# Two dense graph products: byte counts moving past a stationary float32r table, in place of bf16 counts stationary and a bf16 table moving

## What is computed

```python
# layer A: Gaussian mixture convolution over edges, then SiLU, residual and layer norm
gauss  = exp(sum_a(-0.5 * (attr - mu)**2 / (EPS + sigma**2)))         # edges x 3
msg    = einsum('eko,ek->eo', (x[src] @ g).reshape(E, 3, 64), gauss)
aggr   = segment_sum(msg, dst) / max(cnt, 1)
x      = layernorm(x + silu(aggr + x @ root_w + bias + x))
# layer B: two SAGE convolutions over the same edges
def sage(h, W_self, W_neigh, b):
    mean = segment_sum(h[src], dst) / max(deg, 1)
    return h @ W_self + mean @ W_neigh + b
h      = relu(sage(x, W_self1, W_neigh1, b1))
x      = layernorm(x + sage(h, W_self2, W_neigh2, b2))
```

## Time and profile before

| | us |
|---|---|
| median of 3 runs (8571.0 to 8632.7) | 8616.2 |
| span of the profiled execution, first to last instruction | 7138.9 |
| of it up to the end of the count stage | about 5273 |
| fix-up, layer A's end, table | about 194 |
| dense product n = 0 | 827 |
| dense product n = 1 with the end | 845 |

### The profile page before, as it was taken

One profiled execution on the slowest core, in us unless ns is written; L12 is line 12 of the kernel. 1 busy time (PEld: TensorE's weight loads), 2 busy tenths in 40 slices (PEclk: granted clock), 3 DMA queues, 4 the chain that ended last, 5 costly groups with the idle time before them and its releaser, 6 DMA issues.

```text
span 7138.9 us, 141917 instructions
## 1 busy us (share of the span) xinstructions
PE 4916.9 (69%) x35195; PEld 3933.0 (55%) x35196; DVE 4364.6 (61%) x15089; ACT 2701.0 (38%) x8318; POOL 3409.5 (48%) x3146
## 2 busy tenths in 40 slices
PE   1466666666666655566666665565647999999999
PEld 1123444444444433444444444444437999999999
DVE  5667787777777776777777766666645222222222
ACT  3112554554555543455554455555532000000000
POOL 5013776677766665677777777777720000000000
PEclk5556888888888887788888878888867999999999
DMA  3001222222222222222222222222234999999998
GB/s 77 30 25 48 92 83 92 82 97 97 78 95 78 96 78 72 94 96 96 95 77 96 95 97 87 91 94 97 96 92 157 382 380 383 380 368 385 384 385 341
DMA packets 258332, 1082.60 MB, mean 152 GB/s; under 512 B 140102, under 2 KB 144230, under 8 KB 194406
## 3 DMA queue, kind: packets, MB, share of 16 engines
q1 hardware_dynamic: 139588, 965.46, 34.6%
q0 software_dynamic: 100352, 102.96, 6.4%
q10 hardware_dynamic: 18120, 11.31, 0.7%
HBM read 751.67 MB, written 327.81 MB: 151 GB/s over the span
## 4 chain that ended last, share of the span: by engine, by line
PE 39%; DVE 19%; issue 14%; POOL 11%; DVEq 10%; ACT 4%; DMA 2%; ACTq 0%; SPq 0%; POOLq 0%
PE pw L983 22%; POOL rE L498 11%; PE pw L809 9%; DVE rE L1283 5%; PE pw L834 3%; DVEq L1316 3%; DVEq L1492 2%; DVE rE L1343 2%; PE pw L781 2%; DVE rE L1281 2%; ACT rE L545 2%; DVE rE L1411 1%; ACT rB L584 1%; DMA rE<-in_x,idx 1%; DVEq L1268 1%
## 5 line engine op out<-in xcount | busy, mean ns | idle before, releaser
L498 POOL DMA_INDIRECT rE<-in_x,idx x3136 | 3407.4, 1087 | 1828.5 <-issue 1745.6
L809 PE MATMUL pw<-rE 128*128 128x193 f32 x7824 | 1688.3, 377 | 863.1 <-DVE rE L1343 810.2
L584 ACT CAST rB<-pw 128x792 bf16<-128x792 f32 x1568 | 1257.2, 813 | 2509.8 <-PE pw L834 1151.1
L809 PEld LDWEIGHTS pw<-rE 128*128 128x128 f32 x7824 | 1539.5, 222 | 1064.5 <-DVE rE L1343 985.5
L545 ACT ACTIVATE rE<-rE,cols 128x64 f32<-128x64 f32 x4704 | 1255.4, 345 | 8.1 <-DMA tab<-tab_d 8.1
L834 PE MATMUL pw<-rE 128*128 128x396 f16 x3840 | 809.8, 358 | 487.1 <-DVE rE L1283 440.6
L1283 DVE TENSOR_SCALAR rE<-iperm,gr 128x392 f16<-128x392 f16 x3840 | 1051.3, 313 | 0.1
L834 PEld LDWEIGHTS pw<-rE 128*128 128x128 f16 x3840 | 370.1, 103 | 865.9 <-DVE rE L1283 532.0
L983 PE MATMUL pw<-rB,rA 128*128 128x192 bf16 x9604 | 810.7, 246 | 0.1
L983 PE MATMUL pw<-rE,rA 128*128 128x192 bf16 x9604 | 810.5, 246 | 0.1
L983 PEld LDWEIGHTS pw<-rB,rA 128*128 128x128 bf16 x9604 | 790.7, 98 | 1.6
(11 more groups left out here) (258 smaller groups left out, 2550.8 us busy)
## 6 DMA issues: line engine op xcount, KB each, us to landing
rA<-count SPq DMA_DIRECT2D x392, 1568.0 KB, 8.4
count<-rB SPq DMA_DIRECT2D x98, 3136.0 KB
rE<-in_x,idx POOLq DMA_INDIRECT x3136
cols<-cols_d SPq DMA_DIRECT2D x98, 64.0 KB
cols_d<-rA SPq DMA_DIRECT2D x3, 1568.0 KB, 5.2
rA<-in_edge_attr ACTq DMA_DIRECT2D x1, 4608.0 KB
out<-gcol ACTq DMA_DIRECT2D x97, 32.0 KB, 5.7
count<-rB SPq DMA_DIRECT2D x8, 224.0 KB, 2.0
```

Source lines behind the costliest of these rows:

```text
L498: pool.indirect_dma_start(out=gath[:, s, u * CB + b, :], out_offset=None, in_=x, in_offset=bass.IndirectOffsetOnAxis(ap=idx[:, s, u * CB + ...
L584: act.copy(stage[:, s, :, j * 2 * W:(j + 1) * 2 * W].rearrange("p h (w n) -> p w h n", w=2), pu[j % 3][:, :, 0:CW].rearrange("p w (h n) -> ...
L809: ins = pe.matmul(sums[side][:, 0:AW], onehot[:, side, bb, :], wgath[:, side, bb, :], start=(bb == 0), stop=(bb == CB - 1))
```

## The change

Counts become bytes. `stage` is uint8 with four slots, and ScalarE's cast of L584 writes bytes. The bound columns of `comp` hold 1/16 and 1/2048 instead of 1, so that their sums fit a byte, and the limit becomes 240. `count` is laid out by chunks of TC = 4 destination tiles: [4 planes, chunk, 128, ROWB], in which a partition's row is sixteen blocks (`SPANS`: fourteen of 6 groups of src, two of 7), each block holding 4 tiles x 6 (or 7) groups x 128 counts. A tile is stored with two DMAs of runs of 768 and 896 bytes. The fix-up makes three digits by shifts of an int32, and stores each with two DMAs; GpSimd clears a slot of `stage` beforehand.

The table has two pieces instead of three, in float32r: the value with its low 12 bits cleared, and the rest, so `TW` is 128. Now the table is the stationary operand, [128 src, 2 x 64], and the counts of 4 tiles move, 512 columns; the sum is [2 x 64, 512 dst], transposed. [...]

The epilogue runs on a chunk of four tiles: `summed` adds the own rows' pieces, `turn` transposes two tiles at once, ScalarE copies the 512 columns of sums and 256 of own rows (`copied_out`), and `apply` makes eight f32 products of 64 columns. The stacked neighbour weights add the two pieces. 1 / degree is applied behind it, as is the bias, on 256 elements. Output DMAs are issued by GpSimd, one for four tiles. The first block groups of n = 1 are widened while the last two chunks of n = 0 are finished.

```diff
-TW = 3 * D
+TC = 4
+NC = (NT + TC - 1) // TC
+TW = 2 * D
-PARTS = ((0, 26), (26, 24), (50, 24), (74, 24))
+PARTS = ((0, 24), (24, 24), (48, 24), (72, 26))
+SPANS = [(6 * b, 6) for b in range(14)] + [(84, 7), (91, 7)]
+GROUPS = 4
+SHARE = ([3 if b in (3, 7, 11, 13) else 4 for b in range(16)],
+         [3 if b in (2, 3, 6, 7, 10, 11, 13) else 4 for b in range(16)])
...
-                sp.dma_start(tile_of(count[part][0], ORDER[q] - PARTS[part][0]), stage[:, q % 2, None, 0:NT, :]).then_inc(a_st[q % 2], 16)
+                c, t = divmod(ORDER[q] - PARTS[part][0], TC)
+                sp.dma_start(sixes(part)[:, 0, c, t], stage[:, q % 2, 0:84, :].rearrange("p (b h) n -> p b (h n)", h=6)).then_inc(a_st[q % 2], 16)
+                sp.dma_start(sevens(part)[:, 0, c, t], stage[:, q % 2, 84:NT, :].rearrange("p (b h) n -> p b (h n)", h=7)).then_inc(a_st[q % 2], 16)
...
+            def load_counts(part, c, n):                       # SyncE
+                for g in range(GROUPS):
+                    with sp.Fori(0, planes, 1) as pl:
...
+                        for b in range(4 * g, 4 * g + 4):
...
+                            sp.wait_ge(d_conv, free)
+                            sp.wait_ge(a_conv, free)
+                            sp.dma_start(cring[:, b % 4, None, None, 0:size], ...).then_inc(d_ld[b % 4], 16)
...
+            def converted(n, g, tiles):                        # ScalarE
...
+                    for b in range(4 * g, 4 * g + 4):
+                        act.wait_ge(a_eaten, free + b % 4)
+                        act.wait_ge(d_ld[b % 4], landed)
+                        size, d = SPANS[b][1], SHARE[n][b]
+                        act.activation(aring[...], cring[...][:, :, d * P:size * P],
+                                       ACT.Copy, scale=scl[:, bass.ds(k, 1)]).then_inc(a_conv, 1)
...
-                                ins = pe.matmul(pb[s][:, 0:TW], ring[:, s, hi, :], table[:, hi].rearrange("p c d -> p (c d)"),
-                                                start=False, stop=False, skip_group_check=True)
+                                pe.wait_ge(d_conv, done)
+                                for j in range(d):
+                                    ins = pe.matmul(sums_c, table[:, h + j].rearrange("p c d -> p (c d)"),
+                                                    dring[...][:, :, j, :], start=False, stop=False, skip_group_check=True)
+                                ins.then_inc(d_eaten, 1)
+                                pe.wait_ge(a_conv, done)
+                                for j in range(size - d):
+                                    ins = pe.matmul(sums_c, table[:, h + d + j].rearrange("p c d -> p (c d)"),
+                                                    aring[...][:, :, j, :], start=False, stop=False, skip_group_check=True)
+                                ins.then_inc(a_eaten, 1)
...
+                    for t in range(tiles):                     # apply
+                        pe.matmul(pb[4 + s][:, t * D:(t + 1) * D], sT[:, s, t * P:(t + 1) * P], weights[:, 2, :], start=True, stop=True)
+                        ins = pe.matmul(pb[4 + s][:, (TC + t) * D:(TC + t + 1) * D], xT[:, s, t // 2 * P:(t // 2 + 1) * P],
+                                        weights[:, t % 2, :], start=True, stop=True)
...
-                    link(V.tensor_copy(T1[:, lo:hi, 0, :], h0))
+                    link(V.tensor_scalar(h1.bitcast(I32), h0.bitcast(I32), 12, 12, ALU.logical_shift_right, ALU.logical_shift_left))
-                    link(V.tensor_tensor(h1, h0, T1[:, lo:hi, 0, :], ALU.subtract))
+                    link(V.tensor_copy(T1[:, lo:hi, 0, :], h1))
-                    link(V.tensor_copy(T1[:, lo:hi, 1, :], h1))
-                    link(V.tensor_tensor(T1[:, lo:hi, 2, :], h1, T1[:, lo:hi, 1, :], ALU.subtract))
+                    link(V.tensor_tensor(T1[:, lo:hi, 1, :], h0, h1, ALU.subtract))
...
+            def step(n, c, s, tiles=TC, first=False):          # VectorE
+                converted(n, 0, tiles)
+                if not first:
+                    (hidden, residual_of)[n](c - 2, s)
+                converted(n, 1, tiles)
+                if n and not first:
+                    normed(c - 2, s, ...)
+                summed(n, c, s, tiles, first and not n)
+                converted(n, 2, tiles)
+                converted(n, 3, tiles)
```

More of the change, by code:

```diff
@@ L28 @@
 CB = KB // U
-HB = NT // 2
 HP = NT + 1
@@ new lines, in turn @@
+                def turn(c, s, tiles=TC):
+                    pe.wait_ge(x_sum, c + 1)
+                    pe.sem_inc(s_tick[0], 1)
+                    for k in range(tiles // 2):
+                        ins = pe.transpose(pb[2 + s][:, k * P:(k + 1) * P], xs[:, s, 2 * k:2 * k + 2, :].rearrange("p t d -> p (t d)"), ident[:])
+                    ins.then_inc(p_turn, 1)
+                b0 = n * NC
+                dense(n, made={0: 18, 3: NC} if n else {})
+                turn(b0, n)
+                dense(1 - n)
@@ new lines, in _ @@
+                apply(b0, n, first=not n)
+                turn(b0 + 1, 1 - n)
+                with pe.Fori(0, (NC - 3) // 2, 1) as i:
+                    for k in range(2):
+                        s = (k + n) % 2
+                        dense(s)
+                        apply(i * 2 + (b0 + k + 1), 1 - s)
+                        turn(i * 2 + (b0 + k + 2), s)
+                rest_t = NT - TC * (NC - 1)
+                dense(n, rest_t)
+                apply(b0 + NC - 2, 1 - n)
+                turn(b0 + NC - 1, n, rest_t)
@@ new lines, in residual_of @@
+            def residual_of(c, s, tiles=TC):
+                applied(1, c, s, tiles)
+                z = zt[:, 0:tiles, :]
+                V.tensor_tensor(z, z, ht[:, 0:tiles, :], ALU.add).then_inc(d_st, 1)
+                dve.wait_ge(d_st, c * 4 + (4 * NC + 3))
+                dve.sem_inc(s_tick[3], 1)
+                for t in range(tiles):
+                    ins = V.bn_stats(bst[:, t, :], zt[:, t, :])
+                ins.then_inc(d_st, 1)
+                dve.wait_ge(d_st, c * 4 + (4 * NC + 4))
+                dve.sem_inc(s_tick[3], 1)
+                for t in range(tiles):
+                    ins = V.bn_aggr(bag[:, t, :], bst[:, t, :])
+                ins.then_inc(d_var, 1)
@@ new lines, in _ @@
+            step(0, 0, 0, first=True)
+            step(0, 1, 1, first=True)
+            with dve.Fori(0, (NC - 3) // 2, 1) as i:
+                for k in range(2):
+                    step(0, i * 2 + (k + 2), k)
+            step(0, NC - 1, 0, last)
+            converted(1, 0, TC)
+            hidden(NC - 2, 1)
+            hidden(NC - 1, 0, last)
+            converted(1, 1, TC)
+            summed(1, 0, 1, TC)
+            converted(1, 2, TC)
+            converted(1, 3, TC)
+            step(1, 1, 0, first=True)
@@ L1761 @@
+            for c in (2, 3):
+                step(1, c, (c + 1) % 2)
+            with dve.Fori(0, (NC - 5) // 2, 1) as i:
+                for k in range(2):
+                    step(1, i * 2 + (k + 4), 1 - k)
+            step(1, NC - 1, 1, last)
+            residual_of(NC - 2, 0)
+            normed(NC - 2, 0, 16 * 11)
+            residual_of(NC - 1, 1, last)
+            normed(NC - 1, 1, 16 * 12, last)
 _INS = ["x", "src", "dst", "edge_attr_3", "L0_gnn_g", "L0_gnn_mu", "L0_gnn_sigma", "L0_gnn_root_w", "L0_gnn_bias",
```

499 lines of the change are left out of this document (289 added, 210 removed).

## The result

The change makes the kernel faster: 8212.9 us, the median of five runs (8199.1 to 8277.3), against 8615.9 for the kernel before on the same chip (8571.0 to 8632.7). The ratio of the runs is 0.959 with a 95% interval of 0.9554 to 0.9626, which stands for 322 to 384 us; the medians are 403 apart. The forecast was 8165 us, a saving of 451. Later runs of both kernels on a chip with less scatter give a saving of 368 us.

A forecast was written before the change was run, and what follows sets the result against it. TensorE and DMA were taken to bind the dense products level. These were to fall from 1672 to 1211 us (-461), with +10 ahead of them, giving -451 and 8165 us; own range 8060 to 8260, with milder rivals 8040 to 8330.

The forecast's parts named there:

- Columns: Dense products on TensorE: float32r matmul of 512 columns at one column a cycle, 216 ns, 98 of them 21.2 us a chunk.
- the rival of two cycles: Dense products: a float32r column costs two cycles, 44 us a chunk, +510 us, 9125 in all; chance 0.06.
- register work: Group loops of the dense products: added 0.6 us a chunk in layer 1 and 1.4 in layer 2.
- Widening: Byte counts to float32r in the dense products: VectorE 1.20 us per 2048 elements, ScalarE 1.04 per 1024, start to start.
- the rival of one byte a cycle: VectorE's widening reads one byte element a cycle: 37.7 us a chunk, +210 us, 8825 in all; chance 0.05.
- Loads: 384 KB count loads on four buffers: issue 0.5, landing 2.8, widening 1.3, 4.6 of 5.8 us, covered by 1.2.
- the third rival: Ring of loads binds in the dense products: landing 5.5 us, 29.2 us a chunk, -206 us, 8410; chance 0.14.
- Hand-over and tail: Dense products' start, hand-over between layers and longer tail of four tiles: 25 us added.
- what could go wrong: TensorE's clock falls to 1.2 GHz from idling at each hand-off: 21 us a chunk would become 42.
- Before the dense part: Stages ahead of the dense products: fix-up +14 us, table's last step -4, byte evacuation of counts 0.
- the rival of the count stage: Evacuating counts as bytes is twice as slow, a fifth of it on the path: +200 us, 8365; chance 0.05.
- The offset: Median of runs, 8616.2 us, lies 1477 above the profiled span; unexplained and kept constant in the forecast.

The follow-up runs named there:

- The float16 kernel: Changed kernel with table pieces and widened counts in float16 instead of float32r, still four load buffers: 8208.3 us, 0.951 of before; dense products 1289.6 us.
- the ring out of the way: Eight load buffers (two rings of four) instead of four: changed kernel in float32r 8166.1 us, dense products 1246.8; in float16 8098.0 us, dense products 1175.7.
- the float16 kernel with two rings: Changed kernel with float16 tables and widened counts and eight load buffers as two rings of four: 8098.0 us, 0.9425 of before; dense products 1175.7 us.
- the kernel with the other share of the widening: Changed kernel with VectorE widening four tiles of every block, before three in some: 6799.6 us on a quicker chip, 0.951 of before; dense products 1315.9 us.
- the kernel of parts: Separate kernels without the computation, only runs of matmuls, conversions and loads: float32r matmul of 512 columns 227 ns, lone 384 KB load 2.9 to 3.0 us.
- the second trace of before: Kernel before, unchanged, profiled again on the chip of the other runs: span 8636.1 us, execution 8638.0 us; dense products start at 6964.

## Why the prediction was right, and where it missed

**The sign and the mechanism** were right: half the streamed columns a node, TensorE and DMA relieved together. 379 us less in the dense products (1672 to 1293), where 461 were forecast; the miss of 82 us is all there. The time stayed inside the range, and VectorE and ScalarE with their widening did keep up with TensorE wherever loads did not hold them. (The range's lower end, "8080 is TensorE's 23.2 with nothing added, less 20", is a slip: 8616 - 1672 + 49 x 23.2 + 25 + 10 - 20 is 8096.)

**Columns.** About one column a cycle, so the rival of two cycles (0.06) did not come. But 216 ns was the price of a bf16 matmul, and a float32r one takes 233: 98 x 0.017 = 1.7 us a chunk, 82 us over 49. That equals the whole miss to the microsecond, and it would have been easy to stop there. The float16 kernel shows that it is not the whole cause: with the product at 216 ns the dense part still takes 1290 us. What the term is worth is read with the ring out of the way, 1246.8 against 1175.7, 71 us. Against the forecast's 1211 it is 36, since the forecast had 0.6 and 1.4 us a chunk added for register work, of which the float16 kernel with two rings shows nothing in layer 1 (23.13 us a chunk, 23.2 without the addition) and 0.8 in layer 2 (23.97). The rest of TensorE's term was right: the 23.13 us are 98 x 0.216 and 2.0 for apply, transposes and zero matmul, as costed.

The Trainium skill's FP8 and Floating Point Precision (TensorE Precision Notes) lists four passes for true FP32, and for reduced FP32 only that the four bytes are read and truncated. The runs agree, for no pass is added, but they add 11 to 17 ns a matmul of 512 columns (227 to 233 against 216) that the page does not mention.

**Widening.** Right: starts 1.20 and 1.04 us apart, both as forecast, so the rival of one byte a cycle (0.05) is out. With the deeper ring the epilogues are covered as costed: with products at 216 ns, layer 2 beats at 23.97 us, where VectorE was put at 22.8 plus its loops.

**Loads: the step that failed.** The forecast called the round trip of a buffer "covered, by 1.2 us", and held, apart from that, that a ring of four blocks (5.8 us) covers VectorE's epilogue. Both steps spend the same 5.8 us. The first was already short: "384 KB on that line in about 2.8" is right for a load alone, 2.9 to 3.0 us, but with two or three in flight it is 3.6 to 4.0, in the kernel 3.9. The forecast's own sum then reads 0.5 + 3.9 + 1.3 = 5.7 us of the 5.8, and the cover of 1.2 us was 0.1. The second fails on top of it, because while VectorE does the epilogue of a chunk it widens nothing and frees no buffer. A chunk of the float16 kernel in layer 1, VectorE alone:

```profile
7316.64 1.02 DVE L1843 TENSOR_SCALAR dring<-rA,scl 128x1536 f16<-128x1536 uint8 x1 [0.19 <-DMA rA<-count]
7317.57 0.42 DVE L1864 TENSOR_TENSOR gcol<-pw,tri 128x256 f32<-128x256 f32 x1
...
7320.35 0.43 DVE L1889 TENSOR_TENSOR T<-gcol,T 128x256 f32 x1 [0.24 <-DVE T L1886]
7320.82 4.61 DVE L1843 TENSOR_SCALAR dring<-rA,scl 128x2048 f16<-128x2048 uint8 x4
```

From 7317.57 to 7320.82 VectorE is away. By the issues and landings of the same trace the load of block 4 was issued at 7314.06 and landed at 7318.05; ScalarE had widened its part by 7320.10, VectorE only by 7322.11, and the next load into that buffer was issued at 7322.51: a round trip of 8.45 us.

In the steady part of layer 1 (medians) the loads of blocks 4 to 7 lie 2.2 to 3.0 us before VectorE takes them, those of the other twelve at most 0.3, and the round trips are 7.2 to 8.6 us against 5.0 to 6.2. Each buffer is loaded four times a chunk, and a round trip takes 6.32 us on average: 4 x 6.32 = 25.3, the beat of 25.35. In layer 2, where the epilogue is longer and in two parts, blocks 4 to 7 lie for 2.3 to 3.4 us and blocks 8 to 11 for 0.4 to 1.2, and 4 x 6.58 = 26.3, the beat of 26.27. The changed kernel has the same averages within 0.02 us. In the kernel with the other share of the widening the time for which loads lie grew in just these groups, in layer 2 from 3.0 to 3.5 and from 0.7 to 1.3 us on average (0.5 + 0.6 us for a beat that is 0.9 longer).

So the third rival, given 0.14 and 27 to 29 us a chunk, was right that the ring binds, and wrong in how: it had the landing at 5.5 us, where it is 3.9 and the rest is VectorE's absence. It is the other 46 of the 82 us. The forecast's own sign for it, loads that land near 3 us and short waits for a DMA on VectorE, came out against the forecast: 3.9 us, and waits of 142 us in all.

A lone load of 384 KB in 3.0 us is 131 GB/s, and with six and eight of them in flight windows over the kernel of parts have 357 and 364 GB/s. The Trainium skill's DMA: Bandwidth & Descriptors (Bandwidth) asks for at least 1 MiB a DMA for 75% of the peak. For a lone load this case agrees, 131 against 364 GB/s; that overlap brings the rate back and makes each load later is what these runs add.

**Hand-over and tail**, 25 us: right, as 1293 less 1268. It holds a stretch that the prediction named as what could go wrong, on a small scale. Windows at the start of layer 2:

```profile
7616.00:7620.00 4.00, 1.92 (x9) 1.21 (x7) 2.98 (x11) 3.68 (x4) 0.00 (x0) 1.00 0.60 190
7620.00:7626.00 6.00, 5.26 (x12) 4.14 (x13) 5.37 (x6) 2.70 (x2) 0.00 (x0) 0.50 0.58 183
```

TensorE was idle for half of 4 us, and for the next 6 the granted clock was 0.50, its level of 1.2 GHz: 12 matmuls in 6 us. In the steady part the clock stays at 1.00, with TensorE busy 454 of 457 us in layer 1, and in the float16 kernel also where it is busy only 428 of 473 us.

**Before the dense part.** +10 forecast. On the quicker chips the dense products start at 5476.4 and 5466.8 in the profiled executions, so +10, and the medians have 368 us saved against 384 in the dense products (1672 to 1288.0), so +16. A part of the fix-up (first and last of its four starts 6796.01 and 6842.28) takes 15.4 us against 11.1 in the second trace of before (6789.85 and 6823.04): 4 x 4.3 = 17, forecast 14. Evacuation as bytes costs the same, 814 ns against 813 in the earlier trace rows:

```profile
L650 ACT CAST rB<-pw 128x792 uint8<-128x792 f32 x1568 | 1258.7, 814 | 3797.6 <-remote 1104.1
```

so the rival of the count stage (0.05) is out. On the chips that need 8600 us this part scatters by 50 to 60 us between executions (8590 to 8650 for the kernel before on one chip) and can't be read finer.

**The offset.** "1477 above the span ... I keep it constant" was right in number and wrong in place: it is not around the span (a profiled execution takes 2 us more than its span) but in a count stage that is that much slower on the timed chip. It did no harm because the change touches little there; had it touched the count stage, the prices of that trace would have been those of another chip.

In short: 1211 us forecast for the dense products, 36 more for the matmul (71 for its real price, less 35 that the forecast had allowed and the kernel did not need), 46 more for the ring, 1293. The forecast was close because its allowance for register work covered half of the matmul's price; that is luck. The two don't add up freely either. The higher of two floors is paid, 24.93 (TensorE) and 25.35 us (ring) a chunk in layer 1, 25.01 and 26.27 in layer 2, so taking the matmul's 17 ns away alone gave 4 us.

## What to carry to other kernels

Price a load on a ring by its landing with as many in flight as the beat asks for (landing over the time between two loads; 2.5 here, with four buffers and with eight), not by a lone one. Count the round trip as issue, landing and use, and add the longest time in which a user is away: the slack of a ring can be spent once. When the overrun equals one mis-sized term to the microsecond, still take that term away by experiment: here two floors lay within 2 to 5% of each other, and taking away the matmul's extra time alone gave 4 us, both 118. A profile whose span does not match the timed median is of another condition, and the difference has to be placed before prices are taken from it.

## What the hardware showed that was not expected

- A float32r matmul has a floor: 109 to 111 ns for anything from 64 to 192 columns, where float16 takes 56 at 128 and 29 at 64. Its weight load was recorded at 188 ns, that of float16 at 98. At 512 columns it costs 5 to 8% more than float16 (227 to 233 against 216).
- The landing of a 384 KB load grows with the number in flight: 3.0, 3.6, 4.0, 4.5, 5.8 and 7.8 us for one, two, three, four, six and eight. Work of the other engines beside it changes nothing that shows (4.5 at four in flight with and without).
- The chips used here differ by 1470 us in this kernel's count stage and by under 1% in its dense products (1671.9 and 1672 us for the kernel before, 1293.2 and 1288.0 for the changed one).
